# Perceiver block: key parts stored once per chunk, batch 0 handled first, and seven products of ones at the start of TensorE

## The reference, cut to what matters

```python
q = (ln(x) @ Wq.T + bq)   # heads: (B, 16, 128, 8)
k = (ctx @ Wk.T + bk)     # (B, 16, 2048, 8)
v = (ctx @ Wv.T + bv)
attn = softmax(q @ k.T / sqrt(8) + mask)
x = x + (attn @ v) @ Wo.T + bo
x = x + ssm(ln(x), W_in / max(sigma, 1), W_out / max(sigma, 1), ...)
x = x + mlp(ln(x), binarised w1, w2)
```

## Time and profile before

| what | value |
|---|---|
| median of three runs | 326.34 us |
| the profiled execution, whole | 329.18 us |
| its span (first to last instruction) | 327.40 us |
| TensorE matmul busy | 257.0 us (79%) |
| VectorE (DVE) busy | 231.3 us (71%) |
| ScalarE (ACT) busy | 200.7 us (61%) |
| GpSimd (POOL) busy | 108.2 us (33%) |
| mean granted clock of TensorE | 0.895 |

### The profile page before, as it was taken

One profiled execution on the slowest core, in us unless ns is written; L12 is line 12 of the kernel. 1 busy time (PEld: TensorE's weight loads), 2 busy tenths in 40 slices (PEclk: granted clock), 3 DMA queues, 4 the chain that ended last, 5 costly groups with the idle time before them and its releaser, 6 DMA issues.

```text
span 327.4 us, 9590 instructions
## 1 busy us (share of the span) xinstructions
PE 257.0 (79%) x3904; PEld 160.6 (49%) x3904; DVE 231.3 (71%) x425; ACT 200.7 (61%) x309; POOL 108.2 (33%) x267
## 2 busy tenths in 40 slices
PE   0799615499999999999999999999999877550276
PEld 0577401245555556555565655555655444440156
DVE  4358839267878788787878989879888940538941
ACT  1267700267777777877777777777876665195042
POOL 7123421115434553345433665232113120104210
PEclk9999955569999999999999999999999996785559
DMA  6926979941535415344263312311321000000001
GB/s 146 381 88 220 226 179 292 363 153 50 148 92 153 146 50 161 107 127 145 52 188 102 103 50 77 73 50 50 80 68 52 3 4 2 0 0 0 0 0 32
DMA packets 24565, 34.48 MB, mean 105 GB/s; under 512 B 2444, under 2 KB 19112, under 8 KB 24392
## 3 DMA queue, kind: packets, MB, share of 16 engines
q1 hardware_dynamic: 23716, 33.37, 35.0%
q0 software_dynamic: 128, 0.14, 0.5%
q10 hardware_dynamic: 676, 0.33, 0.3%
HBM read 20.20 MB, written 13.63 MB: 103 GB/s over the span
## 4 chain that ended last, share of the span: by engine, by line
PE 58%; ACT 17%; SPq 6%; DMA 6%; DVE 6%; issue 5%; POOL 2%; POOLq 0%; ACTq 0%; DVEq 0%
PE ps L447 15%; ACT probs L739 13%; PE ps L434 13%; PE ps L418 6%; PE ps L320 4%; PE ps L357 4%; SPq L259 4%; PE ps L487 3%; PE ps L495 3%; DMA k_rows_dram<-k_parts 2%; DMA w_kv<-in_L_xattn_Wq_dram 2%; PE ps L455 2%; PE ps L667 2%; PE ps L340 2%; DMA ctx_buf<-in_ctx_dram 1%
## 5 line engine op out<-in xcount | busy, mean ns | idle before, releaser
L1191 DVE TENSOR_REDUCE pmax<-ps 128x2 f32<-128x1024 f32 x128 | 156.1, 1224 | 42.8 <-PE ps L418 41.0
L739 ACT ACTIVATE probs<-ps 128x1024 f32<-128x1024 f32 x128 | 130.8, 1022 | 47.2 <-PE ps L434 47.2
L447 PE MATMUL ps<-probs,v_now 128*9 128x128 f32 x2048 | 82.4, 280 | 0.2 <-ACT probs L739 0.2
L434 PE MATMUL ps<-q_max,k_rows 51*128 51x128 bf16 x1024 | 52.3, 223 | 13.9 <-ACT probs L739 12.8
L447 PEld LDWEIGHTS ps<-probs,v_now 128*9 128x9 f32 x2048 | 43.8, 91 | 34.9 <-issue 33.1
L418 PE MATMUL ps<-k_rows,q_now 48*128 48x512 bf16 x256 | 51.2, 398 | 11.0 <-DMA k_rows<-k_rows_dram 8.3
L968 POOL CAST max_cols<-negmax 128x2 bf16<-128x2 f32 x32 | 6.1, 192 | 133.6 <-DVE negmax L1197 133.6
L434 PEld LDWEIGHTS ps<-q_max,k_rows 51*128 51x128 bf16 x1024 | 30.0, 96 | 37.5 <-ACT probs L739 22.7
L418 PEld LDWEIGHTS ps<-k_rows,q_now 48*128 48x128 bf16 x256 | 12.8, 96 | 14.2 <-DMA k_rows<-k_rows_dram 8.5
L690 ACT ACTIVATE ctxT<-ps 128x512 f32<-128x512 f32 x16 | 9.6, 597 | 14.2 <-PE ps L320 14.2
L357 PE MATMUL ps<-power 128*128 128x128 f32 x96 | 16.7, 297 | 0.2 <-DVE power L1119 0.2
(11 more groups left out here) (184 smaller groups left out, 360.0 us busy)
## 6 DMA issues: line engine op xcount, KB each, us to landing
k_rows<-k_rows_dram SPq DMA_DIRECT2D x64, 192.0 KB, 3.3
k_rows_dram<-k_parts SPq DMA_DIRECT2D x16, 384.0 KB, 3.8
ctx_buf<-in_ctx_dram SPq DMA_DIRECT2D x16, 256.0 KB, 5.5
k_rows_dram<-k_parts SPq DMA_DIRECT2D x16, 256.0 KB, 3.7
k_rows_dram<-k_parts SPq DMA_DIRECT2D x16, 128.0 KB, 4.1
mask_sb<-in_mask_1x1xSxS_ff_dram SPq DMA_DIRECT2D x1, 1024.0 KB, 9.3
q_all<-q_rows_dram SPq DMA_DIRECT2D x2, 384.0 KB, 6.5
w_nat<-in_L_ffn_w_dram SPq DMA_DIRECT2D x2, 256.0 KB, 8.8
```

What stands on the lines that cost most here:

```text
L434: t = pe.matmul(dst, k_rows[rows, i % 4, at:at + P], q_max[rows, i % 2, :], start=not masked, stop=True, skip_group_check=masked)
L447: t = pe.matmul(ps[at:at + HEAD_COLS, 6, 0:P], v_now[:, i % 2, 4 * c + j, HEAD_COLS * h:HEAD_COLS * h + HEAD_COLS], probs[:, c, h, P * j:P ...
L739: act.activation(probs[:, u % CHUNKS, :, :], ps[:, 4:6, :], ACT.Exp).then_inc(probs_ready, 1)
L1191: dve.tensor_reduce(pmax[:, i % 2, :, c], ps[:, bank:bank + 2, :], AX.X, ALU.max).then_inc(pmax_ready, 1)
```

## The change

Key parts go to DRAM once, 24 rows for each head (8 dimensions x 3 parts), by one DMA a chunk. A load of a head writes these 24 rows twice into `k_rows`, by a broadcast, and the first parts' 8 rows once more: 56 rows in place of 48, four DMAs a pair. The queries' layout follows. The head handles batch 0 alone (4 chunks); the queries of batch 0 are projected, split, stored and loaded ahead of the others'. Chunks 4 to 7 are turned and projected between the first scores, and POOL splits them in its loop behind `split_max(0)` to `split_max(3)`; the split of chunks 8 to 15 comes two pairs later than before. Half of the first pairs' loads are issued by POOL. All 24 squarings are in the loop, four in eight units, with the Gram product in unit 55. `q_now` and `v_now` are gone: the matmuls read `q_all` and `v_all`. Seven products of `ones` run first on TensorE. `ctx_buf` has six slots. In the mask's test ScalarE sums magnitudes. Weight means and signs move to DVE's units 42 and 44.

```diff
-SQ_PERIOD = 3
-TINY = 1e-30
+SQ_PERIOD = 4
+TINY = 1e-36
...
+    EARLY = CHUNKS
+    CTX_SLOTS = 6
-    EARLY_SQUARES = 6
+    WARM_UP = 7
+    RAY_UNITS = SQUARE_UNITS + 2 * SQUARINGS
...
-    K_GROUPS = ((0, 3), (3, 2), (5, 1))
-    BLOCKS = 6
-    ROWS = HD * BLOCKS
+    TRIPLE = HD * PARTS
+    ROWS = 2 * TRIPLE + HD
-    LOADS = 32
+    LOADS = 16 * 4
...
-        q_now = sb("q_now", [P, 4, T], BF16)
-        ctx_buf = sb("ctx_buf", [P, FIRST, 4, D])
-        ctxT = sb("ctxT", [P, 2, 512])
+        ctx_buf = sb("ctx_buf", [P, CTX_SLOTS, 4, D])
+        ctxT = sb("ctxT", [P, EARLY, 512])
-        k_32 = sb("k_32", [P, 2, 512])
+        k_32 = sb("k_32", [P, 4, 512])
...
-        v_now = sb("v_now", [P, 2, KT, 2 * HEAD_COLS])
...
+        def store_k(eng, n):
+            b, c = divmod(n, CHUNKS)
+            eng.dma_start(k_dram[b, :, :, 512 * c:512 * c + 512], k_parts[:, :, 512 * n:512 * n + 512]
+                          ).then_inc(k_stored[b % 2] if b else k_first[c], 16)
+
+        def load_half_pair(eng, i, h, keys, loaded):
+            b, p = divmod(i, PAIRS)
+            at, first = HALF_ROWS * h, 16 * p + HD * h
+            n = keys.stop - keys.start
+            triples = k_dram[b, first:first + HD, :, keys].rearrange("r i n -> (r i) n")
+            eng.dma_start(k_rows[at:at + 2 * TRIPLE, i % 4, keys],
+                          triples.rearrange("(a m) n -> a m n", a=1).broadcast_to((2, TRIPLE, n))).then_inc(loaded, 16)
+            eng.dma_start(k_rows[at + 2 * TRIPLE:at + ROWS, i % 4, keys], k_dram[b, first:first + HD, 0, keys]
+                          ).then_inc(loaded, 16)
...
             load_ctx(0)
+            sp.dma_start(w_kv[:, 0, :], Wk).then_inc(ld["wk"], 16)
+            for n in range(1, EARLY):
+                load_ctx(n)
+            sp.dma_start(w_kv[:, 1, :], Wv).then_inc(ld["wv"], 16)
+            sp.dma_start(mask_sb[:, :], mask.rearrange("a b q k -> (a b q) k")).then_inc(ld["mask"], 16)
+            for n in range(EARLY, CTX_SLOTS):
+                load_ctx(n)
+
+            def load_pair(i):
+                wait(sp, keyscores_ready, CHUNKS * (i - 3))
+                for h in range(2):
+                    load_half_pair(sp, i, h, all_keys, k_rows_loaded[i % 4])
+
+            def store_chunk(n):
+                sp.wait_ge(k3_ready, n + 1)
+                store_k(sp, n)
+
+            def store_q_parts(tok, done, groups):
+                for part in range(2):
+                    sp.wait_ge(once("q_step"), done + 2 * part + 2)
+                    store_q(sp, part, tok)
+                sp.wait_ge(once("q_parts_ready"), groups)
+                store_q(sp, 2, tok)
+
+            store_q_parts(first_tokens, 0, 1)
+            store_chunk(0)
+            sp.wait_ge(once("q_stored"), 16 * 3)
+            sp.wait_ge(once("q_all_zeroed"), 1)
+            load_q(sp, first_tokens, once("q_loaded"))
+            sp.wait_ge(once("k_ones_ready"), 1)
+            store_chunk(1)
+            for c in range(2):
+                sp.wait_ge(k_first[c], 16)
+                for h in range(2):
+                    load_half_pair(sp, 0, h, slice(512 * c, 512 * c + 512), k_first[c])
+                load_ctx(CTX_SLOTS + c)
+                store_chunk(2 + c)
+            for c in (2, 3):
+                sp.wait_ge(k_first[c], 16)
+                load_half_pair(sp, 0, 0, slice(512 * c, 512 * c + 512), k_first[c])
+            for i in range(1, 4):
+                load_half_pair(sp, i, 0, all_keys, k_rows_loaded[i])
+            for n in range(EARLY, EARLY + 2):
+                store_chunk(n)
+            store_q_parts(rest_tokens, 4, 2)
+            load_ctx(FIRST)
+            load_ctx(FIRST + 1)
...
+            sp.wait_ge(once("q_stored"), 16 * 6)
+            load_q(sp, rest_tokens, once("q_loaded"))
...
+            for n in range(FIRST + 2, FIRST + 4):
                 load_ctx(n)
-            def store_k(n):
-                b, c = divmod(n, CHUNKS)
-                sp.wait_ge(k3_ready, n + 1)
-                keys = slice(512 * c, 512 * c + 512)
-                for first, parts in K_GROUPS:
-                    sp.dma_start(k_dram[b, :, first:first + parts, keys],
-                                 k_parts[:, 0:parts, 512 * n:512 * n + 512]
-                                 ).then_inc(k_stored_rest if b else k_stored_first, 16)
-
...
-                wait(sp, keyscores_ready, CHUNKS * (i - 3))
-                for h in range(2):
-                    sp.dma_start(k_rows[HALF_ROWS * h:HALF_ROWS * h + ROWS, i % 4, :],
-                                 k_dram[b, 16 * p + HD * h:16 * p + HD * h + HD, :, :].rearrange("r i n -> (r i) n")
-                                 ).then_inc(k_rows_loaded[i % 4], 16)
...
-            store_k(0)
-            store_k(1)
-            sp.wait_ge(once("q_parts_ready"), 1)
-            for first, n, part in ((0, 3, 0), (3, 2, 1), (5, 1, 2)):
-                sp.dma_start(q_dram[:, first:first + n, :], q_parts[:, part:part + 1, :].broadcast_to((P, n, TOK))
-                             ).then_inc(once("q_stored"), 16)
-            store_k(2)
...
-            store_k(3)
-            sp.wait_ge(once("k_ones_ready"), 1)
-            sp.wait_ge(k_stored_first, 16 * len(K_GROUPS) * CHUNKS)
-            for i in range(4):
-                load_pair(i)
-            for n in range(CHUNKS, FIRST):
-                store_k(n)
-            small_vectors()
-            for n in range(FIRST, ALL_CHUNKS):
-                load_ctx(n)
+            for n in range(EARLY + 2, FIRST):
+                store_chunk(n)
             for i in range(4, ALL_PAIRS):
                 if i % PAIRS == 0:
-                    sp.wait_ge(k_stored_rest, 16 * len(K_GROUPS) * CHUNKS * (i // PAIRS))
+                    sp.wait_ge(k_stored[i // PAIRS % 2], 16 * CHUNKS * (2 if i // PAIRS == 3 else 1))
                 load_pair(i)
+                if i % 2 == 1 and FIRST + 4 + (i - 5) // 2 < ALL_CHUNKS:
+                    load_ctx(FIRST + 4 + (i - 5) // 2)
                 if i >= 6 and i % 2 == 0 and FIRST + i // 2 - 3 < ALL_CHUNKS:
-                    store_k(FIRST + i // 2 - 3)
+                    store_chunk(FIRST + i // 2 - 3)
...
+            pe.wait_ge(once("ones_ready"), 1)
+            for _ in range(WARM_UP):
+                pe.matmul(ps[:, 7, 0:P], ones[:, :], ones[:, :], start=True, stop=True)
             pe.wait_ge(ld["ident"], 16)
...
+            turn_ctx(0, 0)
+            pe.wait_ge(ld["wk"], 16)
+            turn(ps[:, 2, 0:P], w_kv[:, 0, :])
+            pe.wait_ge(ld["vec_qk"], 32)
+            pe.transpose(ps[:, 2, 3 * P:3 * P + 2], vec_nat[0:2, :], ident[0:2, 0:2]).then_inc(once("kqv_turned"), 1)
+            turn_ctx(1, 1)
+            pe.wait_ge(once("kT_ready"), 1)
+            project_k(4, 0)
+            pe.wait_ge(ld["wq"], 16)
+            turn(ps[:, 2, P:2 * P], w_kv[:, 2, :]).then_inc(once("kqv_turned"), 1)
+            pe.wait_ge(once("xn_ready"), 1)
+            turn_xn(3, 0, 1)
+            turn_ctx(0, 2)
+            project_k(5, 1)
+            pe.wait_ge(once("qT_ready"), 2)
+            pe.matmul(ps[:, 2, 0:P], kvT[:, 2, :], xnT[:, 0:T], start=True, stop=True).then_inc(once("q_done"), 1)
+            turn_ctx(1, 3)
+            pe.wait_ge(r1_ready, 1)
+            project_k(4, 2)
+            pe.wait_ge(ld["wv"], 16)
+            turn(ps[:, 3, P:2 * P], w_kv[:, 1, :]).then_inc(once("kqv_turned"), 1)
+            pe.wait_ge(r1_ready, 2)
+            project_k(5, 3)
+            pe.wait_ge(once("qT_ready"), 3)
+            project_v(6, 0)
+            project_v(7, 1)
+            pe.wait_ge(r1_ready, 3)
+            turn_ctx(4, 4)
...
+                if i == 0:
+                    pe.wait_ge(k_first[c], 16 + (LOADS if c < 2 else LOADS // 2))
+                    if c == 0:
+                        pe.wait_ge(once("q_loaded"), 16 * 2)
+                    elif c == 2:
+                        pe.wait_ge(second_heads[0], LOADS // 2)
+                elif c == 0:
+                    if i < 4:
+                        pe.wait_ge(second_heads[min(i, 2)], LOADS // 2 if i == 1 else LOADS)
+                    pe.wait_ge(k_rows_loaded[i % 4], LOADS * (i // 4) + (LOADS // 2 if i % 4 else 0))
+                    if i == PAIRS:
+                        pe.wait_ge(once("q_loaded"), 16 * 4)
                 wait(pe, pmax_ready, u - 1)
...
+                k = SQ_PERIOD * m
                 if at == 0:
-                    if m == 0:
-                        pe.wait_ge(v_half_ready, 2 * (ALL_CHUNKS - FIRST))
-                    else:
-                        pe.wait_ge(fro_inv_ready, 2 * (k // SQ_PERIOD) + 1)
-                    square(7, k)
+                    pe.wait_ge(fro_inv_ready, 2 * m + 1)
+                    square(k)
                 elif at == 1:
                     pe.wait_ge(pow_ready, k + 2)
                     side_turns(i)
                 elif at == 2:
                     side_taken(i)
-                    square(7, k + 1)
```

(96 more changed lines are left out.)

550 lines of the change are left out of this document (249 added, 301 removed).

## The result

The changed kernel takes 441.56 us, median of 4 runs (440.62 to 441.82); the kernel before, in the same comparison, 326.67 (326.28 to 327.78). The ratio is 1.350, 95% interval 1.346 to 1.354. I had predicted 339.6 in a range of 330 to 347: the sign was right, the size was off by 102 us. The loss is 114.9 us, more than eight times the 13.3 us that I had summed. The profiled execution has a span of 440.0 us.

What follows compares the result with a forecast made beforehand. It took TensorE (58% of the span) as the bound, with time to win ahead of unit 0 and loop waits paid in full. Terms -9.6 + 12.2 + 8.8 + 1.9 = +13.3 on 326.34 gave 339.6 us, range 330 to 347.

Steps and rivals of the forecast that it cites:

- landing 3.3: In the loop: the last large load of a pair into k_rows lands 3.3 us after its issue.
- Part 3: Loop, odd pairs 7 to 21: loads behind a chunk's store, 1.1 us late eight times, +8.8 (3 to 13).
- Part 2: Loop, pair 4's load behind stores of chunks 6 and 7: wait 9.8, low clock 2.4, +12.2 (10 to 14).
- Part 1: Rewritten head, up to unit 0's side work: start moves from 64.02 to 54.4, -9.6 us (-15 to -6).
- X: Start of unit 0's side work, which turns ctx chunk 8: 64.02 before, forecast 54.4, quickest 49, slowest 58.
- First scores at about 21: Head: the first scores matmul starts at about 21 us, against 48.08 before.
- So scores(2) at 30.5: Head: the third scores start at 30.5 us, after the first two POOL-issued second-head loads land by 30.3.
- Part 4: The loop's other work: six squarings 1.4, Gram product and copies 0.4, norm sum 0.1; +1.9 us (1.4 to 2.5).
- the signs and means: Loop units 42 and 44: 3 us of DVE work cost nothing; without the cover at most 2 us.
- (d): Rival, head: warm-up leaves the clock low; at most 1.5 us, 341.1; inside the forecast, which has chance 0.74.
- (a): Rival, at load_ctx(8) in the head: head wins more than the loop loses; -1.1, or 322.2 us; chance 0.08.
- The signs that I had named: Included, in the loop: one L418 wait of about 10 us for k_rows, then eight of about 1 us.

Runs made afterwards that it cites:

- the form and pair 4 mended: Changed kernel with two 24-row DMAs per repeated pair load, and stores of chunks 6 and 7 behind the loads of pairs 4 and 5; 372.38 us, ratio 1.142.
- the form's run: Changed kernel with only each repeated 48-row pair load written as two DMAs of 24 rows; 388.14 us, ratio 1.182.
- both edits: Changed kernel with each repeated 48-row load as two 24-row DMAs, and the chunk stores moved behind the pair loads; 327.71 us, ratio 1.003.
- three more edits: On both edits: ctx 8 and 9 loaded early, pair 4 early with means and signs spread, pair 5 early; 314.77 us, ratio 0.965.
- The first mend alone: On both edits: loads of ctx chunks 8 and 9 moved ahead of the store of chunk 4; 328.10 us, ratio 1.003.

## Why the prediction was wrong

**The landing of the pair loads** ("landing 3.3", and "Loads of a pair grow from 96 to 112 rows ... so this is hidden"). This is the first step that failed, worth 49 to 53 us. I took the duration of a load whose source and target have 48 rows outermost for one whose source has 2 outermost. Same bytes, 10 us instead of 3.3. The trace of before has no load of that form, so this was a cost to be bounded from both sides, and I treated it as known. What should have stopped me is in the diff, `broadcast_to((2, TRIPLE, n))`. The Trainium skill has the rule, in "DMA: Bandwidth & Descriptors" (Why a DMA increments its semaphore by 16 and not by 1, and Rules for kernel authors): the number of engines is the largest up to 16 that divides the outermost sizes of both patterns, so "a leading zero-stride broadcast of c copies" confines a DMA to at most c engines. The runs agree: a share of 0.15 against 0.125 for two engines, and the packets under way, 16 for the loads of 48 rows, two for those with the repeat, 12 and 8 for those of 24 and 8 rows. The prediction drew on that page for packet sizes only. The rival that this rule makes was missing.

**Part 3, the odd pairs.** The mechanism is right, the size isn't: +8.8 predicted, 44.7 measured (run with the form and pair 4 mended, less the run with both). Its waits are 24.1 us in eight instead of 8.8. The path to the wait of 2.8 in the form's run shows why: from the end of GpSimd's last step at 106.72 to the issue of the last large load, done at 109.67, it takes 2.9 us where I had 1.5. In the changed kernel it is 2.5, with two issues fewer a pair; so the issues themselves were priced too low. The landing is 3.6 for 3.3. The greater error is that I gave the low clock to the long stop of part 2 alone: a wait of 2.8 us is followed by 9.3 us at 0.50, and this slow work makes 20.6 of the 44.7.

**Part 2, pair 4.** +12.2 predicted (10 to 14), 15.8 measured; the wait is 11.8 for 9.8. In the changed kernel it is 17.5; the landing alone is 6.4 longer there (9.95 for 3.53).

**Part 1, the head.** X came at 60.36, not 54.4: -3.7 instead of -9.6, outside the range of -15 to -6. The chain of causes is the one predicted; the wait for ctx chunk 8 is 11.5 us long, and moving its load brought unit 4 forward by 13.4. Two steps of it failed: "First scores at about 21" and "So scores(2) at 30.5". They start at 24.38 and 36.27. First the chain, then TensorE's timeline of the changed kernel, then the third scores with both edits:

```profile
17.61 3.24 DMA k_rows<-k_parts_dram
20.85 3.53 issue
24.38 0.61 PE ps L457 x2
...
24.38 0.61 PE L457 MATMUL ps<-k_rows,q_all 56*128 56x512 bf16 x2 [5.52 <-issue]
24.92 2.07 PE L370 MATMUL ps<-ctxT,kvT 128*128 128x512 f32 x2
...
28.84 1.91 PE L375 MATMUL ps<-kvT,ctxT 128*128 128x128 f32 x8
30.68 0.61 PE L457 MATMUL ps<-k_rows,q_all 56*128 56x512 bf16 x2
...
36.27 0.39 PE L457 MATMUL ps<-k_rows,q_all 56*128 56x512 bf16 x2 [1.56 <-issue]
...
34.63 0.39 PE L457 MATMUL ps<-k_rows,q_all 56*128 56x512 bf16 x2
```

The first keys had landed at 20.85, as predicted, and the profile names nothing for the 3.5 us behind that. The trace's list of instructions does: TensorE's sequencer stands in one instruction from 20.16 to 24.14, the branch on the mask's flag (L711). It takes 3.8 to 4.1 us in the traces of all versions. In the kernel before it takes as long, from 41.77 to 45.83, but there TensorE had to wait for its keys until 48.08, so it was hidden; the change took the cover away, and the prediction has no term for it.

For scores(2) I had the second heads' landing as the bound, at 30.3. In the changed kernel it was indeed the last to come, but at 36.17: these loads have the repeat too. With both edits it came at 32.37 and held nothing; the bound is then TensorE's own order, since it projects chunks 4 to 7 between the scores, 6.6 and 3.6 us for the first two turns, at 0.50 until past 32. I had not put this work into the chain at all. So of the 5.8 us that scores(2) came late, 3.4 were there at the first scores; with the form mended 4.1 are left. The lateness goes on to X, which is 6.0 late.

First projection (6.12 for 7.2) and first query parts (about 11.5 for 12.0) were close. The 1.6 us that the prediction put beside its sum for pieces of 256 bytes did not come: the trace's packets of 256 bytes take 18 ns at the median, those of 512 bytes 27.

**Part 4.** The squarings: from unit 56 to 124 the version with both edits loses 1.7 us against before (113.06 against 111.34), predicted 1.9. But the signs and means, "nothing; without that cover at most 2", cost 3.5 (units 36 to 48: 20.10 us before, 23.60 with both edits): 2.4 of waiting and the low clock again. The cover was one bank of scores; four instructions in one unit, two of them slowed beside GpSimd, are more than that.

**The sum.** The landing 53.4, part 1 6.0, part 2 3.6, part 3 35.9 and part 4 3.3 more than predicted make 102.2, of the 102.0 us that the prediction missed. That they close so well is partly luck, since they come from different versions and single traces.

**Rivals.** (d), the warm-up within 1.5 us, was right for the head; the 2 to 3 us that it seems to cost come later. (a) was nearer than its 0.08 as to place: with X at about 46 and pairs 4 and 5 in time the kernel is faster than before, but this takes three more edits besides the two. The signs that I had named were well chosen: the wait at pair 4 was 17.5 us instead of "about 10", and the later pauses of the loop up to 8.9 instead of 1, and both point at the landing.

## What to carry to other kernels

Read the outermost size of both access patterns of every new or changed DMA before taking a landing time for it from another one: with a repeat outermost, write one DMA per copy. And price a wait of TensorE not by its length: 2.4 to 2.8 us of standing were followed by up to 9 us at the low clock. A wait of 2.8 cost 6.7, and eight of 3.0 on the mean cost 5.6 each, where I had priced 1.1. When a change takes away a long wait, ask what it had covered: here a branch of 4 us. A sync queue that issues the next loads should never stand behind a store that waits for another engine's slow work.

## What I had not expected

- Loads on two engines make other DMAs late too: the last store of a chunk in 12.1 us at the median instead of 4.1, with the DMA engines a tenth busy over most of the stretch.
- Mending one wait moved it: 10.65 us at pair 4, then 4.66 at pair 5, then 2.14 at pair 6, each with its load still behind stores or other traffic in SyncE's queue. The first mend alone was worth nothing (328.10 against 327.71).
- Seven warm-up multiplications brought the first scores 1.3 us forward in both pairs of versions, and unit 0 came 1.6 and 1.25 us later with them. Why the low clock lasts longer there is open.
- VectorE's 128x512 comparison took 0.41 us alone, 0.83 and 1.38 beside GpSimd's steps on the keys. The Trainium skill says in "SBUF — State Buffer" (SBUF: two separate sides) that whichever instruction starts first has the shared pair of ports to its end and the other fully blocks. The trace agrees: L1026 had started first and ended at 124.35, and the comparison beside it ended 0.28 us later.
- A branch on a flag kept TensorE for about 4 us in every trace, and no view of the profile names it; it shows as "issue".
